# Attention opening: where the flag's steps and one projection stand, and unused products on TensorE

## The reference

```python
x = L0_attn_x                                   # (4, 1024, 256)
q, k, v = (einsum('bsm,hmd->bhsd', x, kernel[n]) for n in range(3))   # 16 heads of 64
attn = softmax(einsum('bhsd,bhtd->bhst', q, k) / (64 * 64 * 16), axis=-1)
x = layernorm(x + einsum('bsf,fm->bsm', heads(attn @ v), WO[0]))
x = layernorm(x + ffn(x, ...))                  # 8 experts, top 2, a shared branch
```

## Time and profile before

| | |
|---|---|
| median of 3 runs | 1818.6 us (1818.0 to 1819.65) |
| the profiled execution's own time | 1805.89 us |
| its span, first to last instruction | 1804.1 us |
| mean granted clock of TensorE over the span | 0.98 |
| PE busy | 1722.6 us, 95% of the span |
| DVE busy | 1371.4 us, 76% |
| ACT busy | 1027.3 us, 57% |
| POOL busy | 398.5 us, 22% |

### The profile page before, as it was taken

One profiled execution on the slowest core, in us unless ns is written; L12 is line 12 of the kernel. 1 busy time (PEld: TensorE's weight loads), 2 busy tenths in 40 slices (PEclk: granted clock), 3 DMA queues, 4 the chain that ended last, 5 costly groups with the idle time before them and its releaser, 6 DMA issues. The chain is left out here.

```text
span 1804.1 us, 31876 instructions
## 1 busy us (share of the span) xinstructions
PE 1722.6 (95%) x10919; PEld 1182.8 (66%) x10919; DVE 1371.4 (76%) x2198; ACT 1027.3 (57%) x1529; POOL 398.5 (22%) x442
## 2 busy tenths in 40 slices
PE   6999999999999999999999999899759999999977
PEld 5555555555555555555555555588659999999972
DVE  5888888888888888888888888766666656666647
ACT  5565555556555565655556555466535555555537
POOL 1000000000000000000000000005566777677764
PEclk9999999999999999999999999899869999999998
DMA  5011111111111111311111110356314343333335
GB/s 181 30 36 42 36 42 37 41 36 36 42 36 42 40 38 36 121 48 36 42 42 36 36 42 30 112 193 214 128 67 93 90 88 80 61 91 90 93 60 174
DMA packets 80197, 127.09 MB, mean 70 GB/s; under 512 B 12752, under 2 KB 46736, under 8 KB 77776
## 3 DMA queue, kind: packets, MB, share of 16 engines
q1 hardware_dynamic: 61808, 98.27, 16.2%
q0 software_dynamic: 18272, 27.31, 7.4%
HBM read 86.72 MB, written 38.83 MB: 70 GB/s over the span
## 5 line engine op out<-in xcount | busy, mean ns | idle before, releaser
L447 ACT ACTIVATE a_e<-banks 128x1024 f32<-128x1024 f32 x512 | 483.4, 1032 | 261.6 <-PE banks L344 261.6
L558 DVE TENSOR_TENSOR a_esum<-a_esum,a_e 128x1024 f32<-128x1024 f32 x384 | 470.7, 1226 | 94.2 <-ACT a_e L447 60.4
L358 PE MATMUL banks<-a_e,a_v 128*64 128x512 f32 x2048 | 467.5, 598 | 0.0
L358 PEld LDWEIGHTS banks<-a_e,a_v 128*64 128x64 f32 x2048 | 135.4, 136 | 265.9 <-issue 242.7
L63 POOL MEMSET ident<- 128x128 f32 x1 | 0.2, 205 | 1125.3 <-POOLq L112 1125.3
L344 PE MATMUL banks<-a_qh,a_kh 64*128 64x512 f32 x1024 | 221.3, 427 | 5.7 <-issue 5.3
L344 PE MATMUL banks<-a_qh,a_kl 64*128 64x512 f32 x1024 | 203.4, 390 | 0.0
L344 PE MATMUL banks<-a_ql,a_kh 64*128 64x512 f32 x1024 | 203.1, 391 | 0.0
L1801 ACT ACTIVATE e_g<-banks,e_b1c 128x256 f32<-128x256 f32 x280 | 116.0, 469 | 139.2 <-PE banks L1749 138.6
L344 PEld LDWEIGHTS banks<-a_qh,a_kh 64*128 64x128 f32 x1024 | 96.6, 185 | 145.1 <-issue 97.3
L1762 PE MATMUL banks<-e_w2h,e_hh 128*128 128x256 f32 x560 | 160.6, 287 | 1.0
(11 more groups left out here) (238 smaller groups left out, 3380.9 us busy)
## 6 DMA issues: line engine op xcount, KB each, us to landing
attn_out<-a_ot SPq DMA_DIRECT2D x64, 256.0 KB, 2.0
a_inv<-inv_rows SPq DMA_DIRECT2D x126, 128.0 KB, 2.8
a_w<-w_qkv SPq DMA_DIRECT2D x32, 256.0 KB, 3.1
raw<-attn_out SPq DMA_DIRECT2D x4, 2048.0 KB, 8.9
t_ot<-attn_out SPq DMA_DIRECT2D x4, 2048.0 KB, 9.6
raw<-w_up SPq DMA_DIRECT2D x8, 1024.0 KB, 5.0
raw<-w_down SPq DMA_DIRECT2D x8, 1024.0 KB
raw<-x_t SPq DMA_DIRECT2D x8, 512.0 KB, 9.3
```

The lines of the kernel that those rows point to most:

```text
L358: mm = pe.matmul(o_acc[h * DH:(h + 1) * DH, :], v[quad % 2][:, n, head], e[(slot * ST + n) % NE][:, h * BANK:(h + 1) * BANK], start=n == 0 ...
L447: act.activation(e[t % NE], ring[n % RING], ACT.Exp, scale=SCALE).then_inc(e_ok, 1)
L558: dve.tensor_tensor(acc[:, :], acc[:, :], e[(slot * ST + n) % NE], ALU.add).then_inc(add_ok, 1)
```

## The change

Four things, all in the opening:

- PE issues 18 products that nobody uses (`unused(18)`, 128 x 128 ones by 128 columns of ones, full fp32, into bank 6) ahead of the first unit, once the ones are there; and four more behind the last unit, once seven groups' tops are taken.
- Norm group 7 is made before the last unit and not after it.
- DVE takes the last unit (Q second half) out of its loop: `row_tops(6)` and the flag's chain go ahead of its low part and of `dve_weights(1)`; both follow after the flag, before `dve_weights_v(1)`. PE no longer waits for that low part before the flag; the third score tile of the first slot waits for it, as does the general path.
- Two of the chain's linked steps go: b1 * b1 * wtop is one instruction, and the comparison writes the integer itself.

```diff
@@ names
-        wtop, xtop, b1, b2, b3, flag_f = (inv[0:1, 192 + n:193 + n] for n in range(6))
+        wtop, xtop, b1, b2 = (inv[0:1, 192 + n:193 + n] for n in range(4))
@@ pe_opening
+            def unused(times):
+
+                for _ in range(times):
+                    pe.matmul(x_sum[0][:, 0:P], ones_f, ones_f, start=True, stop=True)
+
+            pe.wait_ge(ones_ok, 2)
+            unused(18)
             for n, u in enumerate(FIRST):
                 pe_unit(pe, u)
                 if n == 4:
                     pe.wait_ge(ones_r_ok, 1)
-                if n >= 4:
+                if 4 <= n < 4 + B * NB - 1:
                     row_norms((n - 4) // NB, (n - 4) % NB)
                 if n == 10:
                     pe.wait_ge(ww_ok, PARTS)
                     wait_evacuated(pe, FIRST[6])
                     pe.matmul(w_sum[:, 0:QK], ones_f, ww, start=True, stop=True).then_inc(w_summed, 1)
-            for u in FIRST[-FIRST_BANKS:]:
+                    row_norms(B - 1, NB - 1)
+            pe.wait_ge(x_top_ok, B * NB - 1)
+            unused(4)
+            for u in FIRST[-FIRST_BANKS:-1]:
                 wait_evacuated(pe, u)
             pe.wait_ge(flag_ok, 1)
@@ pe_bounded, scores
+                if slot == 0 and n == RING - 1:
+                    wait_evacuated(pe, FIRST[-1])
@@ dve_opening
-            for n, u in enumerate(FIRST):
+            for n, u in enumerate(FIRST[:-1]):
                 dve_evacuate(dve, u)
                 if 6 <= n < 6 + PARTS:
                     head_norms(n - 6)
                 if n >= 5:
                     row_tops(n - 5)
-                if n == 10:
-                    dve_weights(dve, 1)
+            row_tops(B * NB - 2)
             dve.wait_ge(w_summed, 1)
...
-            link(dve.tensor_tensor(b2, b1, b1, ALU.mult))
-            link(dve.tensor_tensor(b3, b2, wtop, ALU.mult))
-            link(dve.tensor_scalar(flag_f, b3, LIMIT * LIMIT, None, ALU.is_le))
-            dve.tensor_copy(bounded[:, :], flag_f).then_inc(flag_ok, 1)
+            link(dve.scalar_tensor_tensor(b2, b1, b1, wtop, ALU.mult, ALU.mult))
+            dve.tensor_scalar(bounded[:, :], b2, LIMIT * LIMIT, None, ALU.is_le).then_inc(flag_ok, 1)
+            dve_evacuate(dve, FIRST[-1])
+            dve_weights(dve, 1)
             dve_weights_v(dve, 1)
             dve.wait_ge(flag_ok, 1)
```

## The result

The change makes the kernel faster: 1808.32 us (median of 6, 1807.21 to 1813.03) against 1819.12 for before (median of 6, 1817.01 to 1823.2) in the same runs, a ratio of 0.9945 with a 95% interval of 0.9932 to 0.9957, that is 8 to 12 us less, about 10. In the second comparison (further down) it was 0.9944 again, at other absolute times: 1796.89 against 1807.04. I had forecast 5.0 us less. (Each ratio is estimated from all the runs of its comparison and is not the quotient of the two medians beside it; in microseconds the two differ by up to 1.6.)

The account below looks back on a forecast made before the run. PE, busy throughout attention, was taken as the bound, so the opening's gain carries through: 3.55 us from an earlier start and 1.4 from the clock, taken as -5.0, turn 1818.6 into 1813.6 us; range 1811.5 to 1817.0.

Parts of the forecast that it names:

- The flag's chain: DVE's steps to the flag in the opening: started earlier and two steps shorter, flag at 32.64 against 36.19, -3.55 us.
- What moved behind the flag: DVE's low part of the last projection and second weights, done after the flag: nobody waits for them, 0 us.
- Products ahead of the first projection: 18 unused PE products at the head: no delay, full clock from 9.03, norm group 2 0.35 us earlier, new 2.4 us idle.
- my first rival: Clock falls in the idle before norm group 2 (+2.2 us, 1815.8) or the hole before the scores (1815.0); together 0.22.
- rule of 3 us: Rule from the Trainium skill: no PE idle between bursts should pass some 3 us, so the new 2.4 us idle is harmless.
- Products while the flag is made, and the first slot: Four unused products shrink PE's hole before the first score to 1.4 us, clock stays full: -1.1 to -1.55 us.
- The carrying of the gain through attention: Attention stage, 60 to 1144 us: PE always busy, so whatever the loop's start gains is carried to its end.
- The sum: Whole kernel: 5.0 us less, later stages only shifted, with 1.7 us of spread for their clock; 1813.6 us.
- Profiled time and median: Whole kernel: the median of runs lies 12.7 us above the profiled time, and this difference was assumed to stay.
- The start-up after the flag: Rival, flag to first score: the 1.26 us was partly hidden, up to 2.6 us come back; 1816.9 us, chance 0.12.
- The fall to the low clock one stretch earlier in the token stage: Rival: the 5 us shift makes the clock fall from 1277.5, +10.3 us, 1823.9 us, slower than before; chance 0.05.

Follow-up runs that it names:

- second comparison: The changed kernel run again without edit, against the kernel before in the same runs: 1796.89 against 1807.04 us, ratio 0.9944.
- experiment 1: The kernel before, run again with no edit: median 1806.22 against 1807.04 us, ratio 0.9998.
- experiment 2: The changed kernel, run again with no edit for a second trace: 1796.89 us, ratio 0.9944 to the kernel before.
- experiment 4: The kernel before with only the unused products added, 18 at the head and four before the flag wait: 1802.34 against 1807.04 us, ratio 0.997.
- experiment 7: The changed kernel without the four unused products behind the last projection, the 18 kept: 1798.25 against 1806.04 us for before, ratio 0.9958.
- experiment 10: The changed kernel with five 512-column products for the 18 and one for the four: 1811.52 against 1818.42 us for before, ratio 0.9955.
- experiment 11: The changed kernel with one more one-column product in each of the first 42 slots, 168 instructions: 1821.28 against 1818.42 us for before, ratio 1.0016.
- experiment 12: The kernel before with only 22 one-column products (88 PE instructions) ahead of its first projection: 1816.42 against 1822.11 us, ratio 0.9977.
- experiment 9: The changed kernel with 22 one-column products (88 instructions) at the head instead of its unused products: 1810.4 against 1818.42 us for before, ratio 0.9955.
- experiment 8: The changed kernel with eight more unused products ahead of norm group 2: 1796.75 against 1806.04 us for before, ratio 0.9954.

## Why the prediction was wrong

**The flag's chain** (-3.55 forecast). Flag at 32.80 against 36.19, -3.39; the steps saved were two, and the fused one took 0.21 instead of 0.15. Right.

**What moved behind the flag** (0 forecast). Right: the low part began at 32.73, the first score started 1.26 us after the flag, as before, and DVE's first addition at 37.03 waited for ACT.

**Products ahead of the first projection** (no delay, 0.35 us, and a new idle of 2.4 us). Right in the first trace as to the times: idle 2.26 us, norm group 2 at 21.83. But the 0.35 us aren't the products' doing: experiment 1, the kernel before, reached norm group 2 at 21.91 without them, since its first projection started at 8.63 and not at 9.03. What the profile then decides is whether the clock falls behind that idle, my first rival at 0.22 (with the hole before the scores). It fell in the traces of experiments 2, 4, 7 and 10 and not in those of after and experiment 11: more often than not. Its price was 1.7 us, a little less than the 2.2 I gave it. By the rule of 3 us beside my sum such an idle is harmless; here it was not, and the rows decide.

**Products while the flag is made, and the first slot.** Last exponential at 43.01 against 42.85 forecast; -4.81 for the first slot instead of -4.97. Right.

**The carrying of the gain through attention.** -4.81 became -3.60, with 1.08 us of it lost in one slot. I had read "PE busy 1084.00 of 1084.00" as nothing else being late anywhere; in fact DVE and the queue of the loads were there with little slack left, and a landing 1.2 us later came through to PE. All twelve traces of other kernels than before lose 0.2 to 1.3 us in that slot, and experiment 1 loses none. What makes the landing later wasn't tested: in the traces with 72 to 120 instructions more a code packet starts 7 to 8 us behind the last of these loads, in the others 11 to 12, but the landings of the two groups overlap.

**The sum.** Here the prediction fails: "All of it is shifted by 5 us" is what it says of the later stages, and its spread of 1.7 us for them is for the clock alone. The missing term is the 88 instructions that the 22 products add to PE's program. Their price in time was worked out; their effect on where PE's code packets fall was put at nothing without a reason. It measured 4 to 6 us by experiment 12 alone, and 6 to 8 us in the length of the token stage, as much as all that was meant. With it the sum comes out: 2.9 us from attention and 6.1 from the token stage in experiments 1 and 2, 3.6 and 8.0 in the first traces, are 9.0 to 11.6, measured about 10. How the cost of a packet arises inside a load stays open; that it is the number of instructions and not their work is shown by experiments 9, 11 and 12.

**Profiled time and median.** I carried the 12.7 us over unchanged. That was harmless to the difference, but its likely reason was the experts' stage of 425 or 439 us, not the profile.

**The rivals.** The start-up after the flag did not grow (1.26 us in both). The fall to the low clock one stretch earlier in the token stage did not come.

## What to carry to other kernels

An instruction added to an engine's stream has a second price or prize besides its time: it moves every later code fetch of that engine, and where such a fetch falls into a load that somebody waits for, the load can be late by more than the fetch takes (here 1.1 us of code, up to 2.9 us of landing). When a stage that an edit doesn't touch changes its length, compare in the DMA view whether the code packets lie on its loads, and try the same number of instructions without their work (products of one column) before crediting the edit; empty instructions may not survive the build. A gain of this sort belongs to the alignment and not to the idea: 168 further instructions gave the token stage its old length back and, by their own time in attention, made the kernel slower than at the start.

## What the runs showed of the hardware that I had not expected

- A code packet of 16 KB, about 1.1 us on one DMA engine, that started 1.0 to 1.6 us behind the issue of a 2.5 MB pair of loads went with a landing after 10.6 to 11.8 us in loads 2 to 4 of the stage, over all traces, against 8.7 to 9.8 where it started before the pair or just at its issue.
- The clock fell behind idles of 2.1 to 2.3 us in the middle of dense work in four of six traces before norm group 2 and in three of five before the first score; behind idles of 1.20 to 1.34 us it did in none of seven cases. In experiment 4 it fell 0.6 us after four unused products that stood between idles of 1.54 and 2.56 us. With the first idle filled by unused products (experiment 8) it stayed up.
- The experts' stage has two lengths, 423 to 427 and 437 to 439 us, constant within a comparison, whichever kernel runs. What sets them stays open.
